# A Mamba block and a linear-attention block in one kernel: rows held once, ten state buffers, three products moved, the convolution as matmuls

## The reference

```
xn = layernorm(x) * (1 + scale) + shift           # scale, shift, gate from silu(c) @ ada_w
x_in, z = split(xn @ in_proj)
u = silu(causal_conv(x_in, 4 taps) + conv_b)
dt_r, B, C = split(u @ x_proj);  dt = softplus(dt_r @ dt_proj + b);  A = -exp(A_log)
h[t] = h[t-1] * exp(dt[t] * A) + (dt[t] * u[t]) * B[t]     # per channel, 16 states
y = sum_n h[n] * C[n] + u * D
x = x + gate * ((y * silu(z)) @ out_proj)
xn = ln(x); q, k, v = xn @ Wq, Wk, Wv (+ biases, mask)
q = softmax over each head's 32; k = softmax over time
y = q @ (k^T v);  x = x + silu(ln(y) * (1 + s) + t) @ W_out + b_out   # s, t from silu(c) @ W_emb
```

## Time and profile before

| | |
|---|---|
| median of 3 runs | 666.19 us (665.83 to 669.48) |
| the profiled execution | 668.15 us, of it 666.3 from the first to the last instruction |
| TensorE busy | 452.1 us, 68% of the span |
| VectorE busy | 589.3 us, 88% |
| ScalarE busy | 405.9 us, 61% |
| GpSimd busy | 389.4 us, 58% |
| granted TensorE clock, mean | 0.843 of full speed |

### The profile page before, as it was taken

One profiled execution on the slowest core, in us unless ns is written; L12 is line 12 of the kernel. 1 busy time (PEld: TensorE's weight loads), 2 busy tenths in 40 slices (PEclk: granted clock), 3 DMA queues, 4 the chain that ended last, 5 costly groups with the idle time before them and its releaser, 6 DMA issues.

```text
span 666.3 us, 7102 instructions
## 1 busy us (share of the span) xinstructions
PE 452.1 (68%) x2352; PEld 376.6 (57%) x2352; DVE 589.3 (88%) x618; ACT 405.9 (61%) x874; POOL 389.4 (58%) x292
## 2 busy tenths in 40 slices
PE   3848687678566756778567856776666956775764
PEld 3637566566465645666456745665665756654642
DVE  4809999999999999999999999999999999999321
ACT  2374756558655868387755866487737774754232
POOL 4066759547855786557845694657746696661100
PEclk9978876898689789889689778989789966877886
DMA  7273042002400070005200160007000240000000
GB/s 214 70 248 122 1 162 92 1 16 78 178 1 0 19 268 1 0 17 179 92 0 13 50 226 1 0 16 260 12 0 1 82 190 0 1 16 1 0 16 17
DMA packets 19870, 44.31 MB, mean 67 GB/s; under 512 B 2348, under 2 KB 11060, under 8 KB 19829
## 3 DMA queue, kind: packets, MB, share of 16 engines
q1 hardware_dynamic: 19832, 43.84, 18.9%
HBM read 41.48 MB, written 2.36 MB: 66 GB/s over the span
## 4 chain that ended last, share of the span: by engine, by line
DVE 58%; issue 14%; PE 11%; ACT 9%; POOL 6%; DMA 1%; DVEq 0%; SPq 0%; ACTq 0%; POOLq 0%
DVE ring L635 33%; DVE hs L639 8%; DVE conv L625 5%; POOL hs L383 4%; PE YT L940 3%; ACT ring L504 3%; PE PY L983 2%; DVE st L605 2%; DVE yt L646 2%; DVE kmax L682 2%; PE PX L901 1%; ACT L455 1%; PE PX L836 1%; PE PY L1024 1%; ACT L578 1%
## 5 line engine op out<-in xcount | busy, mean ns | idle before, releaser
L383 POOL TENSOR_TENSOR hs<-dtu,BC 128x1024 f32<-128x1024 f32 x128 | 299.7, 2358 | 107.8 <-PE YT L940 107.7
L635 DVE TENSOR_TENSOR_SCAN ring<-ring,hs 128x1024 f32<-128x1024 f32 x128 | 292.1, 2282 | 20.2 <-POOL hs L383 16.2
L504 ACT ACTIVATE ring<-dt,Aneg 128x256 f32<-128x256 f32 x512 | 213.2, 464 | 149.2 <-DVE hs L639 149.1
L940 PE MATMUL YT<-ident,hs 128*128 128x128 f32 x1024 | 160.0, 312 | 51.5 <-DVE hs L639 51.4
L940 PEld LDWEIGHTS YT<-ident,hs 128*128 128x128 f32 x1024 | 139.9, 163 | 67.6 <-DVE hs L639 62.5
L639 DVE TENSOR_TENSOR hs<-ring,BC 128x1024 f32<-128x1024 f32 x128 | 156.8, 1225 | 4.4
L901 PE MATMUL PX<-xnT,win 128*128 128x256 f32 x232 | 67.0, 439 | 27.2 <-ACT xnT L435 11.2
L901 PEld LDWEIGHTS PX<-xnT,win 128*128 128x128 f32 x232 | 48.8, 222 | 39.9 <-ACT xnT L435 13.6
L983 PE MATMUL PY<-wqkvo,xT 128*128 128x256 f32 x192 | 63.3, 489 | 0.0
L983 PEld LDWEIGHTS PY<-wqkvo,xT 128*128 128x128 f32 x192 | 49.5, 258 | 10.2
L362 POOL TENSOR_TENSOR dt<-dt,conv 128x512 f32<-128x512 f32 x16 | 20.3, 1271 | 53.0 <-ACT conv L484 53.0
(11 more groups left out here) (126 smaller groups left out, 601.4 us busy)
## 6 DMA issues: line engine op xcount, KB each, us to landing
BC<-bc_rows SPq DMA_DIRECT2D x32, 1024.0 KB, 10.1
xg<-in_x SPq DMA_DIRECT2D x8, 256.0 KB, 2.8
out<-fin SPq DMA_DIRECT2D x8, 256.0 KB, 12.3
BC<-in_ada_wT SPq DMA_DIRECT2D x3, 512.0 KB, 5.0
win<-in_in_wT SPq DMA_DIRECT2D x2, 512.0 KB, 6.7
BC<-in_W_emb SPq DMA_DIRECT2D x2, 512.0 KB
wo<-in_out_wT SPq DMA_DIRECT2D x1, 512.0 KB, 13.0
bc_rows<-xdbl SPq DMA_DIRECT2D x8, 32.0 KB, 1.5
```

Of the source, the lines that this page charges most:

```text
L383: nc.gpsimd.tensor_tensor(hs[:, g % DBUF], dtu[:, b % 2, dc, :].unsqueeze(1).to_broadcast([P, NQ, T]), BC[:, b % 2, NQ * q:NQ * q + NQ, :] ...
L504: ins = nc.scalar.activation(ring[:, g % 2, j, :], dt[:, b % 2, dc, :], ACT.Exp, scale=Aneg[:, c:c + 1])
L635: V.tensor_tensor_scan(states, states, driven, 0.0, ALU.mult, ALU.add).then_inc(s_scan_done, 1)
L940: ins = M(YT[:, c, :], hs[:, g % DBUF, j, P * c:P * c + P], ident[:, :], is_transpose=True, start=False, stop=(q == UPC - 1 and j == NQ - ...
```

## The change

- **B and C once.** Br and Cr hold one batch. The DMA of four rows of B for the next batch waits until GpSimd has used these rows for the last time; that of C waits for the last product with them.
- **Ten buffers hs** in place of five. The memory comes from the single Br and Cr and from tiles that share memory.
- **Three of 16 products with C on GpSimd**, those of units 1, 9 and 13 (by_pool). VectorE's scan writes these units' states straight to hs; GpSimd multiplies them, BEHIND = 3 units later in its queue.
- **Convolution as matmuls.** The raw projection is copied to conv, and four matmuls with diagonal weights (diagW, written once by GpSimd) add the shifted copies in PSUM. D * u is a matmul with diagD in YT instead of a copy on ScalarE.
- **z through a second bank**: z is projected with time on the partitions, 512 columns at a time, in bank PZ, while x_in keeps PX.
- **y gated as summed**: VectorE multiplies YT by silu(z) as it copies it out; the transposes follow and a copy on ScalarE (copy_yg) behind them.
- The sum of exp(q) becomes four small matmuls in k_times_v, kmax is negated in its reduction, the gate rows come by DMA, the output is added in x1.
- **The tables**: TensorE sums unit g - 2 in iteration g (LAG), nearly all slots are new, and on ScalarE the decays of unit g come behind the steps of slot g.

The core of the diff (renamed tiles, semaphores and setup left out):

```diff
-DBUF, XBUF = 5, 3
+XBUF, HBUF = 3, 10
+LAG, BEHIND = 2, 3
...
+def by_pool(g):
+    return g % U in (1, 9, 13)
...
+            def broadcast_b(b, q):
+                if b >= 1:
+                    sp.wait_ge(s_dbu_pool, U * b - UPC + q + 1)
+                sp.dma_start(Br[:, NQ * q:NQ * q + NQ],
+                             bc_dram[b % 2, NQ * q:NQ * q + NQ].unsqueeze(0).to_broadcast([P, NQ, T])).then_inc(b_loaded[q], 16)
...
+            def states_times_c(b, i):
+                g, q = U * b + i, i % UPC
+                pool.wait_ge(s_scan_done, g + 1)
+                if i < UPC:
+                    pool.wait_ge(c_loaded[q], 16 * (b + 1))
+                nc.gpsimd.tensor_tensor(hs[:, g % HBUF], hs[:, g % HBUF], Cr[:, NQ * q:NQ * q + NQ, :],
...
                 if 0 <= g < NB * U:
                     inputs_of(g // U, g % U)
-                for slot, step in ((-17, rstd0), (-3, softplus_0), (-1, softplus_1), (24, residual), (26, rstd1),
-                                   (38, rstd2)):
+                if 0 <= g - BEHIND < NB * U and by_pool(g - BEHIND):
+                    states_times_c((g - BEHIND) // U, (g - BEHIND) % U)
+                if g == -20:
+                    setup_diags()
+                for slot, step in ((-21, rstd0), (-4, softplus_0), (-3, softplus_1), (23, residual), (25, rstd1),
+                                   (36, rstd2)):
                     b = due(g, slot)
...
+            def copy_x(b, h):
                 act.wait_ge(s_xz_mm, 4 * b + h + 1)
-                if b >= 1:
+                if b == 0:
+                    act.wait_ge(s_pool_const, 9)
+                else:
                     act.wait_ge(s_dt_sum, 2 * b)
+                nc.scalar.activation(vln[:, 2 * h:2 * h + 2, :], xz_bank(b, h)[:, :, :], ACT.Copy).then_inc(s_xin_ready, 1)
+            def copy_u(b, h):
+                act.wait_ge(s_conv_mm, 2 * b + h + 1)
+                if b >= 2:
+                    act.wait_ge(s_y_acc, U * (b - 2) + U - UPC + 1)
                 for e in range(2):
...
-                    nc.scalar.activation(conv[:, dc, :], xz_bank(b, h)[:, e, :], ACT.Identity, bias=pcol("conv_b", dc, dc + 1),
-                                         scale=pcol("conv_w", TAPS * dc + 3, TAPS * dc + 4)).then_inc(s_conv0_ready, 1)
...
+                    ins = nc.scalar.activation(u[:, b % 2, dc, :], conv_bank(b, h)[:, e, :], ACT.Identity,
+                                               bias=pcol("conv_b", dc, dc + 1))
+                ins.then_inc(s_uraw_ready, 1)
...
-                if g >= 2:
-                    act.wait_ge(s_hc_ready, g - 1)
+                if g >= 2 and by_pool(g - 2):
+                    act.wait_ge(s_scan_done, g - 1)
+                elif g >= 2:
+                    act.wait_ge(s_hc_dve, dve_units(g - 1))
...
+            def copy_yg(b, h):
+                act.wait_ge(s_yg_mm, 2 * b + h + 1)
+                if b >= 1:
+                    act.wait_ge(s_out_mm, b)
+                nc.scalar.activation(yg[:, 2 * h:2 * h + 2, :], PY[:, :, :], ACT.Copy).then_inc(s_yg_ready, 1)
...
-                if 0 <= g < NB * U:
-                    decays(g // U, g % U)
-                for dc in range(DC):
...
-                for slot, step in ((-17, normalize0), (-16, modulated), (-15, conv_last_tap_0), (-14, conv_last_tap_1),
-                                   (-11, copy_z), (-6, copy_xdbl), (-5, softplus_parts_0), (-3, softplus_parts_1),
-                                   (25, normalize1), (26, norm1), (30, exp_qk), (31, mask_v), (32, copy_qT),
-                                   (33, copy_kT), (38, normalize2)):
+                for slot, step in ((-18, normalize0), (-18, modulated), (-17, copy_x_0), (-16, copy_x_1), (-15, copy_u_0),
+                                   (-14, copy_u_1), (-13, copy_z_0), (-12, copy_z_1), (-8, copy_xdbl),
+                                   (-7, softplus_parts_0), (-6, softplus_parts_1),
+                                   (20, copy_yg_0), (21, copy_yg_1), (26, normalize1), (27, norm1), (29, exp_qk),
+                                   (30, mask_v), (31, copy_qT), (32, copy_kT), (37, normalize2)):
                     b = due(g, slot)
                     if b is not None:
...
+                if 0 <= g < NB * U:
...
+                g, q = U * b + i, i % UPC
                 dve.wait_ge(s_da_ready, g + 1)
-                dve.wait_ge(s_dbu_ready, g + 1)
-                driven = hs[:, g % DBUF].rearrange("p n t -> p (n t)")
-                states = ring[:, g % 2].rearrange("p n t -> p (n t)")
-                V.tensor_tensor_scan(states, states, driven, 0.0, ALU.mult, ALU.add).then_inc(s_scan_done, 1)
+                dve.wait_ge(s_dbu_pool, g + 1)
+                decays, driven = flat(ring[:, g % 2]), flat(hs[:, g % HBUF])
...
+            def states_times_c(b, i):
+                g, q = U * b + i, i % UPC
                 dve.wait_ge(s_scan_done, g + 1)
...
+            def gate_y(b, dc):
                 dve.wait_ge(s_y_acc, U * b + UPC * (dc + 1))
-                if b >= 1:
-                    dve.wait_ge(s_yback_mm, 2 * b)
-                V.tensor_copy(yt[:, dc], YT[:, :, :]).then_inc(s_yt_ready, 1)
...
-                for slot, step in ((-23, stats0), (-16, conv_taps_0), (-14, conv_taps_1), (19, gate_y), (21, gate_x),
-                                   (22, stats1), (27, max_qk), (29, sums_qk), (32, head_blocks), (33, normalize_q),
-                                   (34, stats2), (40, finish)):
+                        gate_y(b, dc)
+                if 0 <= g < NB * U and not by_pool(g):
+                    states_times_c(g // U, g % U)
+                for slot, step in ((-22, stats0), (23, gate_x), (24, stats1), (28, max_qk), (30, sum_k),
+                                   (33, head_blocks), (34, normalize_q), (35, stats2), (42, finish)):
                     b = due(g, slot)
                     if b is not None:
                         step(b)
...
+            def convolve(b, h):
+                pe.wait_ge(s_xin_ready, 2 * b + h + 1)
+                if b == 0 and h == 0:
+                    pe.wait_ge(s_diags, 3)
+                    pe.wait_ge(s_pool_const, 9)
+                elif b >= 1 and h == 0:
+                    pe.wait_ge(s_xin_ready, 2 * b + 2)
+                elif b >= 1:
+                    pe.wait_ge(s_uraw_ready, 2 * b + 1)
...
+                    dc = 2 * h + e
+                    dst = conv_bank(b, h)[:, e, :]
+                    for s in range(TAPS):
+                        ins = M(dst, diagW[:, TAPS * dc + s, :], conv[:, dc, s:s + T], start=(s == 0), stop=(s == TAPS - 1))
+                ins.then_inc(s_conv_mm, 1)
...
+                        M(YT[:, c, :], u[:, b % 2, dc, P * c:P * c + P], diagD[:, dc, :], start=(c == 0), stop=False,
+                          skip_group_check=True)
+                if by_pool(g):
+                    pe.wait_ge(s_hc_pool, pool_units(g + 1))
+                else:
+                    pe.wait_ge(s_hc_dve, dve_units(g + 1))
                 for j in range(NQ):
...
-                    sum_states(g // U, g % U)
-                for slot, step in ((-19, transpose_x), (-18, in_proj_0), (-16, in_proj_1), (-14, in_proj_2),
-                                   (-13, in_proj_3), (-9, x_proj), (-8, dt_proj_0), (-6, dt_proj_1),
-                                   (18, transpose_back), (19, out_proj), (23, transpose_x1), (24, q_and_k),
-                                   (28, v_rows), (29, transpose_qk), (31, k_times_v), (31, q_times_att),
-                                   (35, transpose_y), (37, output)):
+                if 0 <= g - LAG < NB * U:
+                    sum_states((g - LAG) // U, (g - LAG) % U)
+                for slot, step in ((-19, transpose_x), (-18, in_proj_0), (-17, in_proj_1), (-16, convolve_0),
+                                   (-15, convolve_1), (-14, in_proj_2), (-13, in_proj_3), (-9, x_proj), (-8, dt_proj_0),
+                                   (-7, dt_proj_1), (20, transpose_yg_0), (21, transpose_yg_1), (22, out_proj),
+                                   (26, transpose_x1), (27, q_and_k), (28, v_rows), (30, transpose_qk), (31, k_times_v),
+                                   (33, q_times_att), (37, transpose_y), (39, output)):
```

485 lines of the change are left out of this document (250 added, 235 removed).

## The result

The changed kernel takes **794.1 us** (median of 4 runs, 792.1 to 796.7), the kernel before, run beside it on the same chip, 666.0: a ratio of 1.191, 95% interval 1.185 to 1.197. The forecast was 775 us, range 700 to 830. The profiled execution took 796.7 us, 794.9 from its first to its last instruction.

A forecast was written before the change was run, and what follows sets the result against it. VectorE was taken as the bound: relieved to 60.6 us a batch, but 27.1 us of queue waits make the period 87.7 instead of 73.3. First scan 59.2, batches 666.5 and tail 49.35 gave 775 us, range 700 to 830.

The forecast's parts named there:

- unit 8, residual: GpSimd's residual, needing VectorE's x1, stands ahead of the eighth unit's inputs; its scan waits 3.8 us a batch.
- unit 10, 1/std, normalize1: Decays queue behind normalize1, which follows stats1 and GpSimd's 1/std chain; VectorE waits 1.95 us a batch.
- maxima of q and k: After unit 12, VectorE waits 5.4 us for q and k, queued on TensorE behind unit 9's sum and GpSimd's product.
- unit 13, exp: On ScalarE, exp of q and k stands ahead of this unit's decays and needs VectorE's subtraction: 3.6 us a batch.
- unit 14, normalize0, modulation, mask: On ScalarE, normalize0, a transpose round trip, modulation and masking of v stand ahead of the decays: 2.7 us a batch.
- unit 17, convolution: Unit 1 of the next batch: copy_u_0 waits for TensorE's convolution ahead of the decays; 4.1 us a batch.
- unit 18: Unit 2 of the next batch: second convolution half and copy_u_1 come before its decays; 1.75 us a batch.
- unit 23, silus: Unit 7 of the next batch: silus and two table loads stand ahead of its decays on ScalarE; 1.9 us.
- units 12, 16, 19, 21: Each loses 0.1 to 1.1 us to similar queue waits, together 1.95 us a batch.
- Rival 1: Ten buffers let the other engines run so far ahead that no meeting is felt: 606 us; chance 0.07.
- Rival 2: Only waits tied by two neighbouring instructions (units 8, 13, 14, 17; 14.2 us) are real: 692 us; chance 0.12.
- Rival 3: TensorE runs the convolution at the low clock: 95 us a batch, about 825 us; chance 0.13.

The follow-up runs named there:

- spaced version: Changed kernel, all parts kept, steps moved one to three units behind what they wait for, decays first on ScalarE, emb operations on GpSimd: 596.7 us, ratio 0.892.
- residual: Changed kernel with only GpSimd's residual addition moved two units later in its order: 787.1 us, ratio 1.177.
- one tap: Changed kernel with one of the convolution's four taps, leaving out 12 of its 16 matmuls a batch: 789.1 us, ratio 1.180.

## Why the prediction was right

*The mechanism.* That the added time is waits at places where queues meet, not work, is shown by the spaced version: same parts, same work (six small emb operations on GpSimd instead of VectorE), 197 us less. VectorE's bare 60.6 us a batch were 60.5 in the changed kernel.

*The waits, by the prediction's terms, as seen in the middle batches:*

| place | forecast | seen |
|---|---|---|
| unit 8, residual | 3.8 | 3.76 |
| unit 10, 1/std, normalize1 | 1.95 | 2.14 |
| maxima of q and k | 5.4 | 4.9 to 5.6 |
| unit 13, exp | 3.6 | 3.16 |
| unit 14, normalize0, modulation, mask | 2.7 | 2.47 |
| unit 17, convolution | 4.1 | 5.4 or 3.8 |
| unit 18 | 1.75 | 1.4 |
| unit 23, silus | 1.9 | 1.6 |
| units 12, 16, 19, 21 | 1.95 | 1.8 |

In three of the four full batches 1.65 us at unit 15 come on top, which the prediction didn't have. The sum of these rows is right, within 1 us a batch. What they are worth one by one is not: 8 x 3.8 us at unit 8 gave 7 us alone (residual), and 2.6 of the 5.4 at unit 17 with all of unit 18's 1.4 gave no shorter period (one tap). The prediction counted each wait once, round the batch, and so got the period; it would have been wrong about nearly any single repair. The one price that came out whole was the maxima's: 32 us for one product, 4.0 a batch.

*Where the 19.9 us between the forecast span (775.05) and the real one (794.9) lie.* First scan +3.0 (62.2 against 59.2), first batch +14.2 (86.2 against 72), second -4.7 (79.8 against 84.5), five full ones -0.3 (438.2 against 438.5), the last +2.0 (73.5 against 71.5), tail +5.6 (54.9 against 49.35). The -0.3 of the five is luck: the forecast has five batches of 87.7, but the four full ones (2 to 5) take 89.0 on average, 1.3 over, mostly unit 15's wait, and batch 6 takes 82.1, 5.6 under, since its second half has no batch 8 to prepare (the kernel before shows the same, 70.6 after 73.4). So the steady period is right to 1.5%, and the two ends are off by more. Of the first batch's 14.2, 6.7 go when the emb operations are moved; most of the rest is a wait of 7.4 us for decays at the second batch's first scan (5.7 with the emb operations moved), which the prediction doesn't have. They stand behind copies of in_proj, which TensorE does late and at the low clock (3.62 us for 8 records). The first scan and the tail are in part clock as well. x_proj takes 3.73 us here and 1.97 in the kernel without products on GpSimd, whose first scan is at 58.3. In the tail out_proj takes 6.19, against 3.72 in the tail before, and TensorE's 132 records 32.7 us against 29.4, which is 3.3 of the 5.6. TensorE in the changed kernel, start and tail, and the same x_proj in the other kernel:

```profile
38.30 3.73 PE L956 MATMUL PX<-u,wxp 128*96 128x256 f32 x8 [3.06 <-ACT u L534]
...
749.01 6.19 PE L1009 MATMUL PY<-wo,yg 128*128 128x256 f32 x16
```

```profile
37.55 1.97 PE L956 MATMUL PX<-u,wxp 128*96 128x256 f32 x8 [3.06 <-ACT u L534]
```

Both x_proj come after the same 3.06 us of waiting, so a single profile tells a first scan only to some 4 us, and the one of the one-tap kernel (55.1) is no proof of a gain there.

*The emb operations* are the term of the sum that was most mis-sized. They were taken at 1 us; the rows show 12.9 us of VectorE (70.23 to 83.15): 8.4 for the four tensor_scalars, which the prediction's sentence on the Trainium skill put at up to 9, and 4.5 for two tensor_tensors, which the prediction left out. The Trainium skill, SBUF — State Buffer, section Who interferes with whom, says that a VectorE instruction in a two-port mode fully blocks against a GpSimd one, and that one with two SBUF inputs contends with a GpSimd one that reads SBUF. The trace agrees: 2.40 us for a tensor_scalar that takes 0.23 at the start, where GpSimd is idle. That it runs in a two-port mode no trace shows. The 0.23 is from this group of the changed kernel:

```profile
L793 DVE TENSOR_SCALAR m0s<-mods,par 128x8 f32<-128x8 f32 x2 | 0.5, 226 | 0.0
```

*The rivals.* Rival 1 (606 us, no meeting is felt) was given 0.07. The spaced version reaches that time, 597, but because its places are others; ten buffers alone don't bring it. Rival 2's list of waits by neighbours was too short: unit 10 and the maxima are as real. Rival 3 asked whether the low clock in the convolution decides; 14 of its 16 halves run at the full one, and with 12 of its 16 matmuls a batch gone the middle periods stay at 88.4 to 89.1. The Trainium skill, TensorE: Matmul & The Clock Gate, section What's actually happening, calls the idling engine the throttled one; the rows agree in direction (granted clock 0.85 with long waits, 0.97 with short ones). How much the low clock adds to VectorE's waits in a full batch of the changed kernel was not measured by itself.

## What to carry to other kernels

When a change takes work off the engine that is the bound, check before anything else how many units each engine stands ahead of what it feeds, in every queue, and what is lined up behind an instruction that waits for the engine being relieved. A small step whose input is just being made must not stand in front of the next unit's inputs: let the urgent work come first and give the small step one to three units of distance. And don't judge a part by removing one wait or by moving one product back: overlapping waits hide each other's price. Here taking all three products off GpSimd made the crowded order 33 us faster, while the spaced order without them, in slots of its own, was 39 us slower.

## What the runs showed of the hardware

- A VectorE tensor_scalar of 128x8 takes 0.23 us alone and 2.40 us while GpSimd's instructions of 128x1024 run back to back; a tensor_tensor of 128x8 with both inputs in SBUF goes from 0.16 to 2.3 (4.56 for two). The same operations on GpSimd take 0.27 and 0.20.
- The scan that writes to SBUF takes 2,280 ns, the one that writes to PSUM 2,293: no difference where up to 0.3 us was allowed for.
- The same 2,656 TensorE records took 529 us in one order (mean granted clock 0.815) and 472 in another (0.921).
